# Masked self-attention on one core: side jobs cut into quarters over a batch's steps, three token buffers instead of two, maxima transposed in the context's bank

## The reference

```python
xt = jnp.transpose(x, (0, 2, 1))
q = xt @ Wq.T
qh = q.reshape(B, T, NH, dk).transpose(0, 2, 1, 3)          # NH = 8 heads, dk = 64
scores = scale * jnp.einsum('bhqd,bhkd->bhqk', qh, qh)       # queries = keys = values
logits = (scores * cmask + (1.0 - cmask) * NEG) * rmask
attn = jax.nn.softmax(logits, axis=-1)
ctx = jnp.einsum('bhqk,bhkd->bhqd', attn, qh)
out = ctx.transpose(0, 2, 1, 3).reshape(B, T, D) @ Wo.T
```

## Time and profile before

| what | us |
|---|---|
| median of 3 executions (1783.22 to 1784.67) | 1784.38 |
| the profiled execution, its own time | 1783.31 |
| its span, first to last instruction | 1781.6 |
| PE busy | 1638.1 (92%) |
| POOL busy | 1358.8 (76%) |
| DVE busy | 1184.3 (66%) |
| ACT busy | 856.5 (48%) |

### The profile page before, as it was taken

One profiled execution on the slowest core, in us unless ns is written; L12 is line 12 of the kernel. 1 busy time (PEld: TensorE's weight loads), 2 busy tenths in 40 slices (PEclk: granted clock), 3 DMA queues, 4 the chain that ended last, 5 costly groups with the idle time before them and its releaser, 6 DMA issues.

```text
span 1781.6 us, 33056 instructions
## 1 busy us (share of the span) xinstructions
PE 1638.1 (92%) x10956; PEld 1252.5 (70%) x10956; DVE 1184.3 (66%) x2704; ACT 856.5 (48%) x2055; POOL 1358.8 (76%) x1165
## 2 busy tenths in 40 slices
PE   6688999999999999989999998999999899999995
PEld 4556777777777777767777777767777677777763
DVE  5347666676767667676676767666676766667673
ACT  1135545463554546455454645545464554546351
POOL 5358787887878788787778878787787877788752
PEclk9679999999999999999999999999999999999997
DMA  3334353443435344353534434353443435344310
GB/s 102 74 81 107 83 138 79 124 103 99 113 86 135 78 125 103 99 119 82 137 76 124 104 99 115 86 136 77 124 104 100 117 83 135 78 120 106 95 49 27
DMA packets 93808, 179.07 MB, mean 101 GB/s; under 512 B 24704, under 2 KB 24832, under 8 KB 93632
## 3 DMA queue, kind: packets, MB, share of 16 engines
q1 hardware_dynamic: 64448, 109.71, 27.1%
q0 software_dynamic: 29184, 67.17, 13.2%
HBM read 36.77 MB, written 33.55 MB: 39 GB/s over the span
## 4 chain that ended last, share of the span: by engine, by line
PE 67%; POOL 12%; issue 9%; DVE 7%; ACT 3%; SPq 0%; DMA 0%; POOLq 0%; ACTq 0%; DVEq 0%
PE misc L1099 20%; PE ctx_psum L1066 15%; PE max_scores L1038 8%; PE scores L1053 8%; PE scores L1056 6%; POOL small_Pacc L554 5%; PE misc L1157 4%; POOL small_xg L488 3%; PE misc L1125 3%; DVE small_mxp L842 3%; ACT small_Pt L712 3%; POOL small_xsum L542 2%; POOL small_idx_cur L481 1%; PE misc L1111 1%; PE misc L1147 1%
## 5 line engine op out<-in xcount | busy, mean ns | idle before, releaser
L842 DVE TENSOR_REDUCE small_mxp<-max_scores 108x1 f32<-108x270 f32 x1280 | 538.8, 435 | 389.2 <-PE max_scores L1038 344.3
L712 ACT ACTIVATE small_Pt<-scores,small_kbias 108x270 f32<-108x270 f32 x1280 | 553.0, 485 | 451.0 <-PE scores L1056 368.8
L554 POOL TENSOR_TENSOR small_Pacc<-small_Pacc,small_Pt 108x540 f32<-108x540 f32 x384 | 534.4, 1392 | 149.6 <-ACT small_Pt L712 141.9
L1038 PE MATMUL max_scores<-small_ops 128*108 128x270 f32 x1280 | 401.4, 332 | 41.1 <-DVE small_mxp L842 36.1
L1066 PE MATMUL ctx_psum<-small_Pt,small_V 108*64 108x270 f32 x2560 | 318.5, 396 | 0.0
L872 DVE RECIPROCAL small_rsum<-small_rsum 128x67 f32<-128x67 f32 (+1 forms) x512 | 241.2, 534 | 115.3 <-ACT small_rsum L658 96.0
L1053 PE MATMUL scores<-small_ops 128*108 128x270 f32 x1280 | 307.0, 306 | 10.1 <-ACT small_Pt L712 8.2
L1038 PEld LDWEIGHTS max_scores<-small_ops 128*108 128x108 f32 x1280 | 220.2, 175 | 128.4 <-issue 59.2
L1056 PE MATMUL scores<-small_ops 128*108 128x270 f32 x1280 | 266.9, 290 | 0.0
L1066 PEld LDWEIGHTS ctx_psum<-small_Pt,small_V 108*64 108x64 f32 x2560 | 191.0, 139 | 107.1 <-issue 5.5
L488 POOL DMA_INDIRECT small_xg<-x_rows,small_idx_cur x160 | 162.9, 1018 | 103.6 <-POOL small_idx_cur L481 44.1
(11 more groups left out here) (106 smaller groups left out, 2242.7 us busy)
## 6 DMA issues: line engine op xcount, KB each, us to landing
small_ops<-small_H SPq DMA_DIRECT2D x512, 135.0 KB
small_ops<-small_L SPq DMA_DIRECT2D x256, 135.0 KB
small_xg<-x_rows,small_idx_cur POOLq DMA_INDIRECT x160
out_rows<-small_xg,small_idx_cur POOLq DMA_INDIRECT x160, 3.2
small_ops<-small_mrow SPq DMA_DIRECT2D x128, 2.1 KB
wq_sb<-wq SPq DMA_DIRECT2D x1, 1024.0 KB, 5.5
woT_sb<-woT SPq DMA_DIRECT2D x1, 1024.0 KB, 8.1
wqT_sb<-wqT SPq DMA_DIRECT2D x1, 1024.0 KB, 10.1
```

Source lines behind the costliest of these rows:

```text
L554: nc.gpsimd.tensor_tensor(acc, other, t["Pt"][:R, p0], ALU.add).then_inc(pacc_step, 1)
L712: nc.scalar.activation(t["Pt"][:R, (NT * h + k) % f.NP, half, :], ST[(2 * (NT * h + k) + half) % 3][:R, 0:H], ACT.Exp, bias=t["kbias"][:R, ...
L842: nc.vector.tensor_reduce(t["mxp"][:R, h % 2, m // 2, m % 2:m % 2 + 1], MX[m % 2][:R, 0:H], AX.X, ALU.max).then_inc(mx_red, 1)
L1038: nc.tensor.matmul(MX[m % 2][:R, 0:H], ops[:, OPA, tile_cols(m // 2)], ops[:, OPB, half_cols(m % 2)], start=True, stop=True).then_inc(mx_r ...
```

## The change

All of it concerns the forms `small` and `middle` (form.split); `small` is the one that runs.

- Projections, output tiles and `w` are cut into quarters (chunks) of 3 matmuls. A step takes one quarter in each part, so that a job of two halves in one step becomes four quarters in two steps (a few keep one step with two quarters in each part). PAIR_STEPS lists first step, last step and job.
- The 5 `xT` stand at (4,0) twice, (4,1) twice and (4,2), and `xv` is made two tiles ahead, the first two at (3,3) and (3,4). `V` moves to (0,3), (4,3), (5,3), (6,3).
- `mT` no longer takes a misc bank: it writes columns 270 to 377 of the context's bank. PE's first value product of a head therefore waits until ACT has read the maxima of the head that follows next.
- Valid token tiles have three buffers, tail tiles one (`xtail`). Gathers of valid tiles move forward to head 0 to 2. `copy_order` is gone, gathers and scatters read `idx` itself.
- Six of the nine token sums a batch move from GpSimd to DVE.

```diff
-PROJ_AT = [(0, 3), (1, 3), (2, 3), (4, 2), (4, 3), (5, 3), (6, 3), (7, 3)]
-V_AT = (0, 1)
-XT_AT = [(3, 1), (3, 2), (3, 3), (3, 4), (4, 0)]
-OUT_AT = [(1, 2), (1, 4), (2, 0), (2, 2), (2, 3)]
-XBAR_AT, W_AT = (7, 1), (7, 3)
+PAIR_STEPS = [
+    ((0, 0), (0, 1), "proj", (2, 1)), ((0, 4), (0, 4), "proj", (3, 0)), ((1, 0), (1, 1), "proj", (3, 1)),
+    ((1, 3), (1, 4), "out", 0), ((2, 0), (2, 1), "out", 1), ((2, 3), (2, 4), "out", 2), ((3, 0), (3, 1), "out", 3),
+    ((3, 3), (3, 4), "out", 4),
+    ((4, 4), (4, 4), "proj", (4, 0)), ((5, 0), (5, 1), "proj", (4, 1)), ((5, 4), (5, 4), "proj", (5, 0)),
+    ((6, 0), (6, 1), "proj", (5, 1)), ((7, 0), (7, 1), "proj", (6, 0)), ((7, 3), (7, 4), "w", 0)]
+V_STEPS = {1: (0, 3), 2: (4, 3), 3: (5, 3), 4: (6, 3)}
+XT_STEPS = [(4, 0, 0), (4, 0, 1), (4, 1, 0), (4, 1, 1), (4, 2, 0)]
+XBAR_STEP = (7, 1, 1)
...
+CTX_HIGH_AT = {(0, 4): 3, (4, 1): 0, (4, 4): 1, (6, 4): 2}
+CTX_LOW_AT = {(1, 1, 0): 3, (4, 4, 0): 0, (5, 1, 0): 1, (7, 1, 0): 2}
...
+ADD_W_AT = [(0, 0), (0, 1), (1, 0), (1, 1), (2, 0)]
+GATHER_AT = [(0, 3), (0, 4), (1, 3), (2, 1), (2, 4)]
+SCATTER_AT = [(2, 2), (3, 0), (3, 3), (4, 0), (4, 3)]
+SCATTER_TAIL_AT = [(1, 4), (2, 3), (3, 1), (3, 4), (4, 1)]
+GATHER_TAIL_AT = [(4, 2), (4, 4), (5, 0), (5, 1), (5, 3)]
+VECTOR_SUM_AT = {1: (5, 0, 1), 2: (5, 1, 0), 3: (5, 1, 1), 4: (5, 4, 1), 5: (6, 0, 1), 6: (6, 1, 0)}
+POOL_SUM_AT = {7: (6, 1), 8: (6, 3), 9: (6, 4)}
...
+    def in_chunks(name, arg, first, last):
+        if first == last:
+            table[first] += [(0, name, arg, (0, 1)), (1, name, arg, (2, 3))]
+        else:
+            table[first] += [(0, name, arg, (0,)), (1, name, arg, (1,))]
+            table[last] += [(0, name, arg, (2,)), (1, name, arg, (3,))]
...
+                def gather(b, k):
+
+                    at_least(pool, scattered[k], 16 * (b + 1 - (f.NB if k < NT else 1)))
...
-                        if arg + 1 < NT:
-                            zero_masked(b + 1, 1 - par, arg + 1)
+                        if arg + f.NA < NT:
+                            zero_masked(b + 1, arg + f.NA)
...
@@ times_values, k == 0
+                        if f.split:
+                            at_least(pe, mrow_done, min(s + 3, HEADS * B))
...
@@ mT
+                        if f.split:
+                            at_least(pe, ctx_done, s - 2)
+                            at_least(pe, mrow_done, s)
+                        row = CT[:NT, H:H + R] if f.split else mb[:NT, 0:R]
```

More of the change, by code:

```diff
@@ L83, in misc_jobs, with whole @@
     table = {(h, k): [] for h in range(HEADS) for k in range(NT)}
-    steps = list(table)
+    def whole(part, name, arg, at):
+        table[at].append((part, name, arg, None))
+    def in_chunks(name, arg, first, last):
[4 more added lines that the diff above has]
+            table[last] += [(0, name, arg, (2,)), (1, name, arg, (3,))]
+    if form.split:
+        for pair, (h, k) in V_STEPS.items():
+            if pair < PAIRS or has_next:
+                whole(0, "V", (pair, 0), (h, k))
+                whole(1, "V", (pair, 1), (h, k))
+        for first, last, name, arg in PAIR_STEPS:
+            if (has_prev if name == "out" else has_next if name == "w" or arg[0] >= PAIRS else True):
+                in_chunks(name, arg, first, last)
+        if has_next:
+            for k, (h, at, part) in enumerate(XT_STEPS):
+                whole(part, "xT", k, (h, at))
+            whole(XBAR_STEP[2], "xbar", 0, XBAR_STEP[:2])
+        for h in range(HEADS):
+            if h > 0 or has_prev:
+                whole(1, "L", h - 1, (h, 2))
+            if h < HEADS - 1 or has_next:
+                whole(1, "mT", h + 1, (h, MT_AT))
+        for jobs in table.values():
+            jobs.sort(key=lambda entry: entry[0])
+        return table
@@ L103, in misc_jobs @@
     for h in range(HEADS - 1 + has_next):
-        table[h, MT_AT].append(("mT", h + 1))
+        whole(1, "mT", h + 1, (h, MT_AT))
     for jobs in table.values():
-        assert all(name not in TWO_PARTS for name, _ in jobs[:-2])
+        jobs.sort(key=lambda entry: entry[0])
     return table
-TWO_PARTS = ("proj", "out", "w")
-LATE = ("proj", "out", "w", "xT")
-def out_steps(form):
-    return OUT_AT if form.NT == 5 else \
-        [(0, 5), (0, 5), (0, 6), (0, 6), (0, 7), (0, 7), (1, 1), (1, 3)]
@@ L181, in with_banks, with bankless @@
 def with_banks(form):
-    def give(jobs, start, two_back):
-        out = []
-        for i, (name, arg, back) in enumerate(jobs):
-            out.append((name, arg, (start + i) % 2, two_back[-2]))
-            two_back = [two_back[-1], (name, arg, back)]
-        return out, two_back
-    def give_table(table, start, two_back):
-        steps = list(table)
-        flat, two_back = give([(*job, 0) for at in steps for job in table[at]], start, two_back)
-        flat = iter(flat)
-        return {at: [next(flat) for _ in table[at]] for at in steps}, two_back
+    def bankless(name):
+        return form.split and name == "mT"
@@ new lines, in give, with give_list, give_table @@
+    def give(job, back, at, two_back):
+        name, arg = job
+        if bankless(name):
+            return None, None, at, two_back
+        return at % 2, two_back[-2], at + 1, [two_back[-1], (name, arg, back)]
+    def give_list(jobs, at, two_back):
+        out = []
+        for name, arg, back in jobs:
+            bank, before, at, two_back = give((name, arg), back, at, two_back)
+            out.append((name, arg, bank, before))
+        return out, at, two_back
+    def give_table(table, at, two_back):
+        out, banks = {}, {}
+        for step, jobs in table.items():
+            out[step] = []
+            for part, name, arg, chunks in jobs:
+                before = None
+                if chunks is None or chunks[0] == 0:
+                    banks[name, arg], before, at, two_back = give((name, arg), 0, at, two_back)
+                ends = chunks is None or chunks[-1] == 3
+                out[step].append((part, name, arg, chunks, banks[name, arg], before, ends))
+        return out, at, two_back
@@ L211, in with_banks @@
-    assert same_end == end
-    last, end = give_table(tables[2], at, one_later(end))
-    tail, _ = give(tail_jobs(form), at + count(tables[2]), one_later(end))
+    front, at, end = give_list(front_jobs(form), 0, [None, None])
+    first, at, end = give_table(tables[0], at, end)
+    start = at
+    mid, at, same_end = give_table(tables[1], at, one_later(end))
+    assert same_end == end and (at - start) % 2 == 0
+    last, at, end = give_table(tables[2], at, one_later(end))
+    tail, _, _ = give_list(tail_jobs(form), at, one_later(end))
@@ L1206, in batch @@
                                 max_scores(s + 2, 2 * b + (h + 2) // SLOTS, h + 2, 2 * k + 1)
-                            for name, arg, bank, before in table[h, k]:
+                            for at, name, arg, chunks, bank, before, ends in table[h, k]:
                                 if name == "L" and f.split:
```

288 lines of the change are left out of this document (137 added, 151 removed).

## The result

The changed kernel takes 1762.04 us (median of four executions, 1761.24 to 1765.23) against 1784.41 before: a ratio of 0.988, 95% interval 0.987 to 0.989. It is faster, as forecast, but by 22 us and not by 84: 1762 lies outside the range of 1650 to 1750. The profiled execution has a span of 1759.9 us, its own time is 1761.67.

A forecast was written before the change was run, and what follows sets the result against it. PE was taken as the bound: 87.0 us of its own work a batch plus 12.1 of losses, 99.1 against 103.95. Fourteen batches save 67.9, the ends 16.9, together 84.8, giving 1700 us; range 1650 to 1750.

The forecast's parts named there:

- Quarters: Short steps: a quarter job in each part covers PE's waits for ACT and DVE; loss 4.6 a batch becomes 0.9.
- (3,0), (3,1): Steps of head 3 where PE waits for DVE's output tiles: output operations spread out, loss 2.9 becomes 0.2.
- `xT`: (4,0) to (4,2): PE waits for `xv` from ACT; loss 2.6 in place of 3.3, bounds 0.6 and 4.
- (4,4): Maxima of (4,4) wait for DVE, whose reciprocals of (4,2) end late: loss 0.9, bounds 0 and 1.5.
- `mT`: A head's value product waits for ACT's copy of the maxima: loss 0.3, bounds 0 and 1.
- (5,2) with (5,3): At (5,2), PE waits for DVE, late from three sums in (5,0), (5,1): loss 1.7, replacing POOL's 1.8.
- Copies of head 8: At (6,0), PE waits for head 8's copies and the maxima behind them: loss 1.1, bounds 0 and 3.
- `xbar` at (7,1): POOL's 75 us a batch, sums included, spread with no head over 11.5: loss 0.
- Ends: Start 4.0 and 2.9, batch 0 8, batch 15 2: 16.9 us gained together, bounds 8 and 25.
- the third: Rival: DVE and POOL hold each other up, six sums and four `ctxT_lo` wait 0.7 more each; 1749 us, chance 0.24.
- its worst case: Exclusion rule at its worst: six sums on DVE wait 1.35 each, 8 us of DVE a batch, most of the gain.
- the 0.17 of the mean of 880: Extra wait for each sum on DVE in (5,0), (5,1), from `ctxT_lo`'s mean 880 ns; 0.4 taken for three.

The follow-up runs named there:

- kernel 5: The changed kernel with VectorE's six token sums of batches 1 to 15 replaced by one-input reductions at the same places; 1743.03 us, ratio 0.978.
- experiments 13 to 15: Five tail-tile gathers earlier: in two kernels with all sums on GpSimd and `ctxT_lo` moved (pair 4 as changed, 1669.60; early, 1665.45), and in the changed kernel, 1753.87.
- kernels 2, 3, 7: The changed kernel with pair 4's projections earlier: alone, 1766.55 us; with three sums back on GpSimd, 1796.71; with all nine sums on GpSimd, 1757.73.
- 15: The changed kernel with only the five gathers of tail tiles earlier; 1753.87 us, ratio 0.982.
- Kernel 14: The changed kernel with all sums on GpSimd, pair 4 early, three of four `ctxT_lo` after k = 2, tail gathers earlier; 1665.45 us, ratio 0.932.

## Why the prediction was wrong, point by point

The losses below are means over batches, from the starts of the steps less the issue that the prediction's rates give the step; what k = 2 and `V` lose in every kernel is taken off.

- **Quarters: right.** (5,0), (0,0), (0,1) and the output steps lose 0.02 to 0.03 each; (6,4) keeps 0.86. The experiment without them gives the size: 60.9 us, where the prediction's term for short steps is 14 x (4.6 - 0.9) = 52. Since that experiment also puts the output tiles' VectorE work closer together, the 60.9 are not the short steps alone.
- **(3,0), (3,1): 0.95, forecast 0.2.** VectorE has scaling and an output tile there still. Not tested alone.
- **`xT`: about 2.6 (2.5 to 2.8), forecast 2.6. (4,4) and `mT`: nothing, forecast 0.9 and 0.3.** (4,0), (4,1) and (4,2) take 1.92, 2.72 and 5.06; 0.31 to 0.36 from start to start for each `xT`, 0.74 for six matmuls and 3.81 for a k = 2 step are taken off. 1.2 better than thought.
- **(5,2) with (5,3): 1.65, forecast 1.7.** That the size came out is luck. It was put together from a late VectorE, 1.3, and 0.4 for three sums that wait, from the mean of `ctxT_lo`, 880 ns. With sums that never wait (kernel 5) the two steps lose 0.7, not 1.3; and the three sums took 1.03, 0.68 and 2.55, 2.2 over their own lengths and not 0.4. The two errors cancel. A mean over `ctxT_lo` in other places says how often *that* operation met GpSimd; on a GpSimd that is busy 74% of the time (1070.30 of 1447.50), a new operation meets it mostly.
- **Copies of head 8: (5,4), (6,0), (6,1) together 4.7, forecast 1.1 (bounds 0 and 3). This is the step that failed**: `small_L` 3.5 after the start of (5,2), six copies in 3.8, the maxima there 2.5 later, 9.8 in all, against PE at (6,0) after 9.0. (9.8 less 9.0 is 0.8; why 1.1 was taken the prediction does not say.) On the mean `small_L` ended 4.48 after the first scores of (5,2) and the first copy was issued at 4.65; six copies took 4.35 to issue, and PE was released 3.3 later, at 12.3. PE had come after 9.46, near the forecast. In batch 6 the parts are 4.48 (779.25 against 774.77), 5.28 (779.42 to 784.70, one issue of 2.19 where 0.6 is usual) and 2.6. Each part was late by about 1, and they add up to a wait of 2.9. The prediction counted neither the tail gathers beside the copies, about 1 us (experiments 13 to 15), nor that PE comes out of the wait at half the clock in 10 of 14 batches, for which (6,0) and (6,1) lose 1.3 on the mean.
- **`xbar` at (7,1): 1.2, forecast 0.** The sentence "three sums at 1.3: 75 us, spread so that no head has more" looked at GpSimd's sum per head, not at the date of the last sum, two additions before (7,1). With sums earlier the wait fell to 1.0 us in the whole run.
- Together (4.7 - 1.1) + 1.2 + 0.75 - 1.2 = 4.35, the 4.3 by which the batch, 103.4, missed 99.1.
- **Ends: 13.9 of the forecast 16.9.** The start gave 7.3 (104.8 to 97.5; forecast 6.9), batch 0 2.3 (forecast 8), batch 15 with its tail 4.3 (forecast 2).

Of the rivals the third named the mechanism (VectorE and GpSimd hold each other up, "lengths of the sums near 1.4") and came closest, 1749; it had 0.24. Its condition was met in part: the six sums took 1.18 on the mean, 0.5 over their own length and not 0.7, and the four `ctxT_lo` almost nothing (a mean of 749 ns). It is a part of the cause: one-input sums give back 19 us of the 62 that were missed. The wait for copies is the larger part. It went in several ways, with pair 4 early (kernels 2, 3, 7) or the gathers elsewhere (15), but time was only won where VectorE was on time as well. Kernel 14, at 1665, shows that the forecast's 1700 could be had from this change with the sums on GpSimd and `ctxT_lo`, pair 4 and the tail gathers placed otherwise.

The Trainium skill ("SBUF — State Buffer", Who interferes with whom) says of this: a VectorE instruction with two SBUF inputs contends with a GpSimd instruction that reads SBUF, one with at most one does not, and whichever issued first holds the shared ports to its end. The runs agree: 673 to 686 ns for 84 one-input reductions, 679 to 2550 for the sums. The prediction weighed two sizes for this, its worst case of 1.35 for each of six sums, 8 us of DVE a batch, and the 0.17 of the mean of 880. The six sums waited 3.0 us a batch in all, 0.5 each, between the two. Most of the gain was lost, as in the worst case, but for the larger part by the copies.
